# A block with adaptive norms, a gated scan and routed experts: three more expert tiles chosen from the counts after six of eight groups

## Chip, cores and metric

One Trainium2 chip, one core. The metric is the device time of one execution in microseconds (us), lower is better. PE is TensorE, DVE VectorE, ACT ScalarE, POOL GpSimd and SP SyncE.

## What is computed

x has 2 sequences of 2048 tokens with 128 features, so 4096 tokens. With the modulation vectors sa, ca, ga, sb, cb, gb from silu(c) @ wmod:

```
h = layernorm(x) * (1 + ca) + sa
x = x + ga * scan(h)                      # gated linear recurrence along a sequence
h = layernorm(x) * (1 + cb) + sb
logits = silu(h @ rw1 + rb1) @ rw2 + rb2  # 8 experts
two largest logits, softmax over these two -> we[token, expert]
out = sum over e of we[:, e] * (silu(h @ w1[e] + b1[e]) @ w2[e] + b2[e])
x = x + gb * out
```

HID is 512. Every token goes to two experts, so 8192 rows pass through an expert.

## The kernel before

**Groups and tiles.** The first part works in 8 groups of 512 tokens: norm (`norm1`), transpose (`turn_x`), gates, scan, transpose back (`turn_y`), residual and second norm, transpose (`turn_h`), router (`router`, `logits`, `sum`), the two largest (`top2`) and the place of each row (`rank`, `place`). POOL then sends the rows of a group to `sorted_rows` in HBM, ordered by expert, with 8 indirect transfers per group (`send:n` in the plan, two token blocks each; L556, 64 in all). The second part works in 39 tiles of 256 rows of one expert each. For tile s, SP loads the rows into one of U = 10 row places of `xr` (L421); PE turns them (`tx`, L1234), DVE copies them to `xT` (L1010) and copies the expert's weights to a working place (`w1` L1019, `w2` L1028, each after reading the expert's number from `tab` into a register); PE does layer 1 (`l1`, L1245), ACT the silu (`hid`, L665), PE layer 2 (`l2`, L1263), ACT the bias (`yb`, L674), PE turns back (`ty`, L1273), DVE scales (`sc`, L1036) and POOL scatters the rows to `expert_out` with two indirect transfers (`scat`, L567). A load into a used row place waits until the scatter of the tile ten before it has landed (L420).

**Which tiles when.** `tab` holds the first row and the expert of each tile. The first EARLY = 9 tiles hold whole tiles that are full once the first four groups are counted: `early_table` (table1, L944) picks them on DVE, and SP loads them behind the sends of groups 0 to 3 (L434 to L438). The rest are listed by `late_table` (table2, L982), `turn_table` on PE (`tturn`) and `table_row` (table3), from counts at four levels: what is left of the first half (`entries`, table1b), groups 5 and 6 (`middle_levels`, table1c, which reads `lev:0` of PE) and everything. SP then writes padding rows behind each expert (L442), waits for the second table and for all sends (L443 to L445) and loads tile 9 and on.

**What sets the order.** The strings of PLAN (L259) give each engine's order, part by part, from the start of the kernel to tile 10 or so. Each engine executes its parts in that order and waits on semaphores. On DVE, parts joined by + take turns, and `link` (L711) makes the next operation of a part wait for the end of the one before. The PE parts around the change wait as follows: `tx:3` writes the bank that `xT:2` reads, so it waits for it; `logits:7` writes the bank of `lev:0`, so it waits for the first operation of table1c (s_levr); `l1:2` needs `xT:2` and `w1:2`. `turnb` (L1099) transposes the expert biases; it waits for the three transfers of `smallb`, issued by ACT at the start (L583 to L585), and for DVE's copy of the first transpose. `warm:n` are matmuls whose result nobody reads.

After the plan, `expert_steps` (L364) runs a loop of 2 rounds of U = 10 tiles from tile FIRST = 11, then the last 8 tiles as straight code. In that straight part the output is summed group by group: SP loads both rows of each token of a group from `expert_out` (`load_y`), DVE combines them with x in three operations (`combine`, L1050), SP stores. SUMS (L371) says behind which step each group is combined.

## Time and profile before

| | us |
|---|---|
| three runs, median (lowest, highest) | 289.26 (288.16, 289.66) |
| the profiled execution, its own time | 288.93 |
| its span | 287.2 |
| PE busy, share of span | 254.2, 89% |
| DVE busy | 188.9, 66% |
| ACT busy | 166.9, 58% |
| POOL busy | 170.0, 59% |

Busy time is what the profiler sees of each engine; a wait is charged to the work that ended last before it. The span counts from the first to the last instruction; the time around it is 1.7 us. PE's share is an average: the slices of the page show it at nine tenths or more from about the fifteenth of forty on, and lower before, when the groups' scan and norms are made. The lines in the rows are those of the kernel before.

### The profile page before, as it was taken

To read this page: it belongs to the slowest core of one execution; us is meant where nothing else is said; L and a number is where in the kernel's file an instruction comes from. 1 tells how busy PE (TensorE), PEld (TensorE's weight loads), DVE (VectorE), ACT (ScalarE), POOL (GpSimd) and SP (SyncE) were. 2 spreads that over 40 slices of the span, in tenths; PEclk is the share of its full clock that TensorE was granted. 3 is DMA by queue.
4 is the path that set the end of the run, shared out by engine and by line. 5 is a ranking of instruction groups with operands and counts; after the bars stand their busy time and mean duration, and the time that the engine had idled before them with its cause. 6 is when DMAs were issued, how large, how long until landed. Compare 5 with 4: busy or idle time off the path is not lost.

```text
span 287.2 us, 4973 instructions
## 1 busy us (share of the span) xinstructions
PE 254.2 (89%) x1187; PEld 177.0 (62%) x1187; DVE 188.9 (66%) x751; ACT 166.9 (58%) x323; POOL 170.0 (59%) x192
## 2 busy tenths in 40 slices
PE   7886997998889997999998999999999999989910
PEld 3343443354244334787877888888888888867800
DVE  3959999999999987576443444444444446868333
ACT  4169999999885445544554555555555555444400
POOL 3994311267777757777777777545554545635650
PEclk9999999999999999999999999999999999999975
DMA  7994010121131226413423433222216822290504
GB/s 212 306 333 126 19 38 26 51 66 59 46 119 54 88 74 154 126 48 111 141 71 107 110 102 110 53 76 75 65 55 194 237 74 74 75 265 4 160 0 146
DMA packets 45365, 30.51 MB, mean 106 GB/s; under 512 B 5085, under 2 KB 41999, under 8 KB 45342
## 3 DMA queue, kind: packets, MB, share of 16 engines
q1 hardware_dynamic: 39888, 21.49, 27.5%
q0 software_dynamic: 4544, 8.47, 8.9%
q10 hardware_dynamic: 910, 0.30, 0.4%
q8 instruction: 8, 0.13, 0.2%
q14 instruction: 15, 0.12, 0.1%
HBM read 16.39 MB, written 12.67 MB: 101 GB/s over the span
## 4 chain that ended last, share of the span: by engine, by line
PE 43%; POOL 23%; issue 14%; DVE 12%; DMA 5%; DVEq 1%; ACT 1%; POOLq 0%; ACTq 0%; SPq 0%
POOL sorted_rows L556 21%; PE bank L1263 18%; PE bank L1245 17%; PE bank L1273 3%; PE bank L1234 2%; DVE st L722 2%; DMA expert_out<-shared,tx 2%; PE bank L1150 1%; POOL shared L520 1%; PE bank L1151 1%; PE bank L1090 1%; DVE tx L816 1%; DVE hT L821 1%; DVE shared L742 1%; DMA xs<-in_L_attn_x_dram 1%
## 5 line engine op out<-in xcount | busy, mean ns | idle before, releaser
L567 POOL DMA_INDIRECT expert_out<-shared,tx x78 | 79.3, 1016 | 54.1 <-DVE shared L1036 37.6
L665 ACT ACTIVATE hT<-bank,w_t 128x256 f32<-128x256 f32 x156 | 65.5, 471 | 29.5 <-PE bank L1245 28.6
L556 POOL DMA_INDIRECT sorted_rows<-rows,sloti x64 | 64.1, 1001 | 27.2 <-issue 18.3
L1263 PE MATMUL bank<-hT,w_t 128*128 128x256 f32 x312 | 74.1, 380 | 0.0
L1245 PE MATMUL bank<-xT,w_t 128*128 128x256 f32 x312 | 74.0, 380 | 0.0
L1245 PEld LDWEIGHTS bank<-xT,w_t 128*128 128x128 f32 x312 | 56.3, 190 | 6.6 <-DVE w_t L1019 0.5
L1263 PEld LDWEIGHTS bank<-hT,w_t 128*128 128x128 f32 x312 | 56.2, 190 | 6.3
L674 ACT ACTIVATE yT<-bank,w_t 128x256 f32<-128x256 f32 x38 | 18.0, 474 | 46.3 <-PE bank L1263 46.3
L1174 PE MATMUL bank<-h2T,rw_s 128*128 128x512 f32 x64 | 33.5, 623 | 1.0 <-ACT qv L652 0.5
L1010 DVE COPY xT<-bank 128x256 f32<-128x256 f32 x39 | 16.4, 422 | 22.4 <-PE bank L1234 22.4
L1036 DVE TENSOR_TENSOR shared<-bank,tx 128x256 f32<-128x256 f32 x38 | 16.1, 424 | 19.7 <-PE bank L1273 19.6
L1028 DVE COPY w_t<-w_s 128x513 f32 x39 | 17.8, 457 | 16.5 <-issue 15.6
L1019 DVE COPY w_t<-w_s 128x516 f32 x39 | 17.3, 443 | 16.1 <-issue 14.9
L1114 PE MATMUL bank<-ident 128*128 128x512 f32 x30 | 17.7, 702 | 2.0 <-POOL ident L492 2.0
L722 DVE BATCH_NORM_STATS2 st<-xs 128x6 f32<-128x128 f32 x64 | 15.7, 282 | 4.5 <-DMA xs<-in_L_attn_x_dram 4.4
L1174 PEld LDWEIGHTS bank<-h2T,rw_s 128*128 128x128 f32 x64 | 10.0, 189 | 12.6 <-issue 5.9
L1234 PE MATMUL bank<-ident,tx 128*128 128x128 f32 x78 | 15.2, 276 | 2.1 <-DMA tx<-sorted_rows 1.4
L1273 PE MATMUL bank<-ident,yT 128*128 128x128 f32 x76 | 14.7, 275 | 1.9 <-DVE xT L1010 1.5
L1234 PEld LDWEIGHTS bank<-ident,tx 128*128 128x128 f32 x78 | 10.4, 141 | 8.0 <-issue 2.5
L1273 PEld LDWEIGHTS bank<-ident,yT 128*128 128x128 f32 x76 | 10.1, 141 | 7.4 <-issue 4.2
L652 ACT ACTIVATE qv<-bank,smallbT 128x512 f32<-128x512 f32 x16 | 10.8, 686 | 6.4 <-PE bank L1174 6.4
L512 POOL TENSOR_TENSOR rs<-ve,half_neg 128x4 f32<-128x4 f32 x8 | 8.6, 1087 | 9.4 <-DVE ve L729 9.4
(198 smaller groups left out, 326.6 us busy)
## 6 DMA issues: line engine op xcount, KB each, us to landing
tx<-sorted_rows SPq DMA_DIRECT2D x39, 130.0 KB, 2.3
w_s<-in_L_ffn_w_dram SPq DMA_DIRECT2D x16, 256.0 KB, 6.0
xs<-in_L_attn_x_dram SPq DMA_DIRECT2D x8, 256.0 KB, 5.3
rows<-rows SPq DMA_DIRECT2D x8, 256.0 KB, 2.6
av<-expert_out SPq DMA_DIRECT2D x8, 256.0 KB, 3.7
qv<-expert_out SPq DMA_DIRECT2D x6, 256.0 KB, 5.3
expert_out<-shared,tx POOLq DMA_INDIRECT x78, 2.4
sorted_rows<-padr SPq DMA_DIRECT2D x9, 130.0 KB, 2.8
```

The costliest lines, as they stand in the source:

```text
L556: p.indirect_dma_start(sorted_rows[:, :], bass.IndirectOffsetOnAxis(ap=sloti[:, k, t:t + 1], axis=0), rows[:, t, k, :], None).then_inc(s_d ...
L567: p.indirect_dma_start(expert_out[:, :], bass.IndirectOffsetOnAxis(ap=xr_i[:, s % U, n, D + 1:D + 2], axis=0), yo[:, s % U, n, :], None, b ...
L665: ins = nc.scalar.activation(hsT[:, u % 2, h, :], bank[4 + q][:, (h % 2) * SL:(h % 2 + 1) * SL], ACT.Silu, bias=w1_t[:, u % 2, HID + h:HID ...
L674: nc.scalar.activation(yT[:, u % 2, :], out_bank(s)[:, 0:SL], ACT.Identity, bias=w2_t[:, u % 2, HC * D:W2E]).then_inc(s_yT_e, 1)
L722: ins = v.bn_stats(st[:, t, :], xs[:, t, :])
L1028: v.tensor_copy(w2_t[:, u % 2, :], w2_s[:, bass.ds(e * W2E, W2E)]).then_inc(s_w2t, 1)
L1114: t.matmul(bank[to][:, :].rearrange("p (k q) -> p k q", q=P), ident[:, :], ident[:, :].unsqueeze(1).to_broadcast([P, 512 // P, P]), start= ...
L1174: t.matmul(bank[2 + n % 2][:, :], rw1_s[:, h * P:(h + 1) * P], h2T[:, g % 2, :], start=True, stop=True).then_inc(s_rl1, 1)
L1234: ins = t.transpose(bank[1][:, n * P:(n + 1) * P], xr[:, u, n, 0:D], ident[:, :])
L1245: ins = t.matmul(bank[4 + h // 2][:, (h % 2) * SL:(h % 2 + 1) * SL], w1_t[:, u % 2, h * P:(h + 1) * P], xT[:, u % 2, :], start=True, stop= ...
L1263: ins = t.matmul(out_bank(s)[:, 0:SL], w2_t[:, u % 2, h * D:(h + 1) * D], hsT[:, u % 2, h, :], start=(h == 0), stop=(h == HC - 1))
L1273: ins = t.transpose(bank[1][:, n * P:(n + 1) * P], yT[:, u % 2, n * P:(n + 1) * P], ident[:, :])
```

## The change

- SLOTS = 12 row places instead of 10. Tiles 0 and 1 use places 10 and 11, tiles 2 to 9 their own number, 10 and 11 places 0 and 1; from tile 12 on a tile uses its number modulo 10, as before. Places 10 and 11 are used once.
- Tiles 9, 10 and 11 (NEXT = 3) are picked by a table of their own, `middle_table` (tablem), from the counts after six groups (`count6`, copied in `place:6` from a new matmul in `rank:6`). `remaining` (tablen) takes them out of the entries of the last table. Both stand on DVE between w1:1 and table1c. table1c now compares one level instead of two.
- SP loads tiles 9 to 11 behind the sends of groups 4 and 5 (s_disp[1]), ahead of the padding. The last table, the padding and the other sends (s_disp[2]) are waited for ahead of tile 12. The loop starts with tile 12, and 7 tiles follow it.
- The plan is longer by one tile; in it DVE does xT:12 and w1:12 ahead of w2:10.
- On PE, turnb:0 moves from behind gates:0 to the place ahead of warm:1 and mod:0.
- Groups 0 to 5 are summed at steps 32 to 36 and 38; before, at steps 31 to 36. Group 6 stays at step 40.

The diff, without the places where `s % U` only becomes `slot(s)` and `(u + 1) % U` becomes `step_slot(s, u, 1)`:

```diff
-    FIRST = 11
+    FIRST = 12
+    SLOTS = 12
...
-    LATE = TILES - EARLY
+    LATE = TILES - FIRST
+    NEXT = FIRST - EARLY
...
-        yo = shared[:, 0:U * SL].rearrange("p (u n d) -> p u n d", u=U, d=D)
+        yo = shared[:, 0:SLOTS * SL].rearrange("p (u n d) -> p u n d", u=SLOTS, d=D)
...
-        xr = tx[:, 0:U * HALVES * ROW].rearrange("p (u n r) -> p u n r", u=U, n=HALVES)
+        xr = tx[:, 0:SLOTS * HALVES * ROW].rearrange("p (u n r) -> p u n r", u=SLOTS, n=HALVES)
...
+        s_disp = sems("s_disp0", "s_disp1", "s_disp2")
...
+        def counted_6():
+            return bank[6][:, 2 * GT * NE + NE:2 * GT * NE + 2 * NE]
...
-                warm:0 turnc:0 warm:1 mod:0 warm:2 turn_x:0 gates:0 turnb:0 turn_x:1 gates:1 turn_x:2 warm:3 turn_x:3
+                warm:0 turnc:0 turnb:0 warm:1 mod:0 warm:2 turn_x:0 gates:0 turn_x:1 gates:1 turn_x:2 warm:3 turn_x:3
...
-                tx:11 l1:10 ty:8 l2:9""",
+                tx:11 l1:10 ty:8 l2:9 tx:12 l1:11 ty:9 l2:10""",
...
-                norm2:7 place:4 table1:0 w1:0 top2:5 place:5 xT:0 xT:1 w2:0 table1b:0+top2:6 place:6 w1:1 table1c:0
-                w1:2 xT:2 xT:3 w1:3 w2:1 rowsB:0 sc:0 w2:2 top2:7 xT:4 w1:4 place:7 w2:3 sc:1 w1:5 xT:5 w2:4 table2:0
-                sc:2 w1:6 xT:6 sc:3 xT:7 w2:5 w1:7 w2:6 sc:4 w2:7 xT:8 table3:0 sc:5 w1:8 w1:9 sc:6 w2:8 xT:9 w2:9
-                w1:10 xT:10 sc:7 xT:11 w1:11 sc:8 w2:10""",
+                norm2:7 place:4 table1:0 w1:0 top2:5 place:5 xT:0 xT:1 w2:0 table1b:0+top2:6 place:6 w1:1 tablem:0
+                tablen:0 table1c:0 w1:2 xT:2 xT:3 w1:3 w2:1 rowsB:0 sc:0 w2:2 top2:7 xT:4 w1:4 place:7 w2:3 sc:1 w1:5
+                xT:5 w2:4 table2:0 sc:2 w1:6 xT:6 sc:3 xT:7 w2:5 w1:7 w2:6 sc:4 w2:7 xT:8 table3:0 sc:5 w1:8 w1:9 sc:6
+                w2:8 xT:9 w2:9 w1:10 xT:10 sc:7 xT:11 w1:11 sc:8 xT:12 w1:12 w2:10 w2:11 sc:9""",
...
-                hid:4 yb:3 hid:5 yb:4 hid:6 yb:5 hid:7 yb:6 hid:8 yb:7 hid:9 yb:8 hid:10""",
+                hid:4 yb:3 hid:5 yb:4 hid:6 yb:5 hid:7 yb:6 hid:8 yb:7 hid:9 yb:8 hid:10 yb:9 hid:11""",
...
+        def counted_7():
+            return turn_bank("lev", 0)[:, 0:NE]
...
         SUMS = {FIRST + ROUNDS * U: 0, FIRST + ROUNDS * U + 1: 1, FIRST + ROUNDS * U + 2: 2,
-                FIRST + ROUNDS * U + 3: 3, MID + 12: 4, FIVE + 5: 5, TILES + 1: 6}
+                FIRST + ROUNDS * U + 3: 3, FIRST + ROUNDS * U + 4: 4, TILES - 1: 5, TILES + 1: 6}
...
-            return (s - u) // U + 1
+            if static(s) and s < SLOTS:
+                return 1
+            return (s - u) // U + 1 if u >= SLOTS - U else (s - u - U) // U + 1
+
+        def step_slot(s, u, by):
+            return slot(s + by) if static(s) else (u + by) % U
+
+        def slot(s):
+            return U + s if s < SLOTS - U else s % U
 
         def landed(eng, last):
-            for u in range(U):
-                eng.wait_ge(s_sc[u], 16 * HALVES * ((last - u) // U + 1))
+            for u in range(SLOTS):
+                eng.wait_ge(s_sc[u], 16 * HALVES * len([s for s in range(last + 1) if slot(s) == u]))
...
-                if not (static(s) and s < U):
+                if not (static(s) and s < SLOTS):
...
-                if s * HALVES * ROW + HALVES * ROW > GPB * G and s * HALVES * ROW <= GPB * G:
+                if s == 0:
                     sp.wait_ge(s_y, NG)
-                load(s, s % U)
+                load(s, slot(s))
+
+            sp.wait_ge(s_tab, 2)
+            sp.wait_ge(s_disp[1], 16 * TOPK * GPB // 2 * GT)
+            for s in range(EARLY, FIRST):
+                load(s, slot(s))
 
             sp.wait_ge(s_pads, 1)
             for e in range(NE):
                 padding(bass.ds(sp.value_load(pad_i[0:1, e:e + 1], min_val=e * REG, max_val=e * REG + TOK), SL))
-            sp.wait_ge(s_tab, 2)
+            sp.wait_ge(s_tab, 3)
             sp.wait_ge(s_pad, 16 * (NE + 1))
-            sp.wait_ge(s_disp[1], 16 * TOPK * GPB * GT)
-            for s in range(EARLY, FIRST):
-                load(s, s % U)
+            sp.wait_ge(s_disp[2], 16 * TOPK * GPB // 2 * GT)
...
-                            rows[:, t, k, :], None).then_inc(s_disp[t // (GPB * GT)], 16)
+                            rows[:, t, k, :], None).then_inc(s_disp[max(0, t // GT - GPB + 2) // 2], 16)
...
+                if g == 6:
+                    yield from link(v.tensor_copy(count6[:, :], counted_6()))
...
+                v.memset(mbase[:, 2 * NE:2 * NE + 1], float(4 * NE * REG))
+                yield from link(v.memset(mval[:, 1, :], 1.0))
+                v.memset(mval[:, 1, NE - 1:NE], float(1 - NE))
...
-                yield from link(v.tensor_tensor(row_0[:, 0:1], row_p[:, 0:1], base[:, 0:1], ALU.add))
+
+            def middle_table(_):
+                yield from link(v.tensor_tensor(cmpk[:, :, :, :], count6[:, :].unsqueeze(2).unsqueeze(3)
+                                                .to_broadcast([P, NE, 2, KT]), kthr[:, :, :, :], ALU.is_gt))
+                v.tensor_copy(mbase[:, 0:NE], base[:, 0:NE])
+                yield from link(v.tensor_reduce(reach6[:, :, :], cmpk[:, :, :, :], AX.X, ALU.add))
+                yield from link(v.tensor_tensor(low[:, :], full[:, :, 0], reach6[:, :, 1], ALU.min))
+                v.tensor_tensor(more[:, 0:NE], low[:, :], taken[:, :], ALU.subtract)
+                v.scalar_tensor_tensor(mbase[:, NE:2 * NE], low[:, :], float(SL), ereg[:, :], ALU.mult, ALU.add)
+                yield from link(v.tensor_tensor(more[:, NE:2 * NE], reach6[:, :, 1], low[:, :], ALU.subtract))
+                v.tensor_tensor(mval[:, 0, :], mbase[0:1, 1:2 * NE + 1], mbase[0:1, 0:2 * NE], ALU.subtract)
+                yield from link(v.tensor_tensor_scan(mupto[:, :], one[:, 0:2 * NE], more[:, :], 0.0, ALU.mult, ALU.add))
+                yield from link(v.scalar_tensor_tensor(mval[:, 0, :], more[0:1, :], -float(SL), mval[:, 0, :], ALU.mult, ALU.add))
+                yield from link(v.tensor_tensor(cmpm[:, :, :], tauf[:, 0:NEXT].unsqueeze(2).to_broadcast([1, NEXT, 2 * NE]),
+                                                mupto[0:1, :].unsqueeze(1).to_broadcast([1, NEXT, 2 * NE]), ALU.is_ge))
+                yield from link(v.tensor_tensor(cmpn[:, :, :, :], cmpm[:, :, :].unsqueeze(1).to_broadcast([1, 2, NEXT, 2 * NE]),
+                                                mval[:, :, :].unsqueeze(2).to_broadcast([1, 2, NEXT, 2 * NE]), ALU.mult))
+                yield from link(v.tensor_reduce(tfm[:, :, :], cmpn[:, :, :, :], AX.X, ALU.add))
+                yield from link(v.tensor_scalar(tfm[:, 0, :], tfm[:, 0, :], mbase[0:1, 0:1], None, ALU.add))
+                v.tensor_tensor(tab[:, :, EARLY:FIRST], tfm[:, :, :], taus[:, :, 0:NEXT], ALU.add).then_inc(s_tab, 1)
+                dve.wait_ge(s_tab, 2)
+
+            def remaining(_):
+                yield from link(v.scalar_tensor_tensor(tk[:, :], mupto[:, :], -1.0, more[:, :], ALU.mult, ALU.add))
+                yield from link(v.tensor_scalar(tk[:, :], tk[:, :], float(NEXT), 0.0, ALU.add, ALU.max))
+                yield from link(v.tensor_tensor(tk[:, :], tk[:, :], more[:, :], ALU.min))
+                v.tensor_tensor(nent[:, 0:NE], nent[:, 0:NE], tk[:, 0:NE], ALU.subtract)
+                v.tensor_tensor(nent[:, NE:2 * NE], reach6[:, :, 0], full[:, :, 0], ALU.subtract)
+                yield from link(v.scalar_tensor_tensor(base[:, 0:2 * NE], tk[:, :], float(SL), base[:, 0:2 * NE], ALU.mult, ALU.add))
+                v.tensor_tensor(row_0[:, 0:1], row_p[:, 0:1], base[:, 0:1], ALU.add)
+                yield from link(v.tensor_tensor(nent[:, NE:2 * NE], nent[:, NE:2 * NE], tk[:, NE:2 * NE], ALU.subtract))
 
             def middle_levels(_):
                 dve.wait_ge(s_lev, 1)
-                v.tensor_tensor(cmpl[:, :, :, :], levels_of("lev").rearrange("p (l e) -> p l e", l=2).unsqueeze(3)
-                                .to_broadcast([P, 2, NE, KT]),
-                                kthr[:, :, 0, :].unsqueeze(1).to_broadcast([P, 2, NE, KT]), ALU.is_gt).then_inc(s_levr, 1)
+                v.tensor_tensor(cmpl[:, :, :], counted_7().unsqueeze(2).to_broadcast([P, NE, KT]),
+                                kthr[:, :, 0, :], ALU.is_gt).then_inc(s_levr, 1)
                 dve.wait_ge(s_levr, 1)
-                yield from link(v.tensor_reduce(reach[:, :, :], cmpl[:, :, :, :], AX.X, ALU.add))
-                v.tensor_tensor(nent[:, NE:2 * NE], reach[:, 0, :], full[:, :, 0], ALU.subtract)
-                v.tensor_tensor(nent[:, 2 * NE:3 * NE], reach[:, 1, :], reach[:, 0, :], ALU.subtract)
-                yield from link(v.scalar_tensor_tensor(base[:, 2 * NE:NENT].rearrange("p (l e) -> p l e", l=2), reach[:, :, :],
-                                            float(SL), ereg[:, :].unsqueeze(1).to_broadcast([P, 2, NE]),
-                                            ALU.mult, ALU.add))
+                v.scalar_tensor_tensor(base[:, 2 * NE:3 * NE], reach6[:, :, 0], float(SL), ereg[:, :], ALU.mult, ALU.add)
+                yield from link(v.tensor_reduce(reach[:, :], cmpl[:, :, :], AX.X, ALU.add))
+                v.tensor_tensor(nent[:, 2 * NE:3 * NE], reach[:, :], reach6[:, :, 0], ALU.subtract)
+                yield from link(v.scalar_tensor_tensor(base[:, 3 * NE:NENT], reach[:, :], float(SL), ereg[:, :], ALU.mult, ALU.add))
                 yield from link(v.tensor_tensor(dbase[:, :], base[:, 1:NENT + 1], base[:, 0:NENT], ALU.subtract))
...
-                v.tensor_scalar(tab[:, :, EARLY:TILES], table_bank().rearrange("p (k s) -> p k s", k=2),
+                v.tensor_scalar(tab[:, :, FIRST:TILES], table_bank().rearrange("p (k s) -> p k s", k=2),
                                 float(NE * REG), None, ALU.min).then_inc(s_tab, 1)
-                dve.wait_ge(s_tab, 2)
+                dve.wait_ge(s_tab, 3)
...
+                if g == 6:
+                    t.matmul(counted_6(), ones_h[:, :], mboth[:, 6, 0, :], start=True, stop=True)
...
-                t.matmul(levels_of("lev").rearrange("p (l e) -> p l e", l=2), ones_h[:, :], mboth[:, 6:8, 0, :],
-                         start=True, stop=True).then_inc(s_lev, 1)
+                t.matmul(counted_7(), ones_h[:, :], mboth[:, 7, 0, :], start=True, stop=True).then_inc(s_lev, 1)
...
-                        layer2(s - 1, (u - 1) % U, lambda: turn_out(s - 2, (u - 2) % U))
+                        layer2(s - 1, step_slot(s, u, -1), lambda: turn_out(s - 2, step_slot(s, u, -2)))
```

## Rows read from the trace of the kernel before

**Rows 1.** The page, part 4: the chain that ended last, shares of the span by line.
```profile
POOL sorted_rows L556 21%; PE bank L1263 18%; PE bank L1245 17%; PE bank L1273 3%; PE bank L1234 2%; DVE st L722 2%; DMA expert_out<-shared,tx 2%; PE bank L1150 1%; POOL shared L520 1%; PE bank L1151 1%; PE bank L1090 1%; DVE tx L816 1%; DVE hT L821 1%; DVE shared L742 1%; DMA xs<-in_L_attn_x_dram 1%
```

**Rows 2.** The chain in order of time: start us, us, what.
```profile
122.92 1.06 POOL sorted_rows L556
...
144.82 1.00 POOL expert_out L567
...
149.22 2.36 DMA tx<-sorted_rows
```

**Rows 3.** Timeline of PE: start us, us, instruction, idle time before it and releaser.
```profile
119.03 1.06 PE L1181 MATMUL bank<-qv,rw_s 128*32 128x512 f32 x8
...
120.11 0.41 PE L1234 MATMUL bank<-ident,tx 128*128 128x128 f32 x2
...
150.03 0.38 PE L1234 MATMUL bank<-ident,tx 128*128 128x128 f32 x2
...
151.62 0.44 PE L1234 MATMUL bank<-ident,tx 128*128 128x128 f32 x2 [1.21 <-DMA tx<-sorted_rows]
...
151.90 1.89 PE L1245 MATMUL bank<-xT,w_t 128*128 128x256 f32 x8
...
155.79 1.89 PE L1245 MATMUL bank<-xT,w_t 128*128 128x256 f32 x8
```

**Rows 4.** Windows, 120.1 to 150: length, busy PE, PEld, DVE, ACT, POOL, clock, DMA.
```profile
120.10:150.00 29.90, 29.09 (x154) 24.48 (x155) 17.60 (x61) 15.75 (x37) 22.78 (x24) 1.00 0.30 92
```

**Rows 5.** Timeline of DVE around the tables.
```profile
116.62 0.43 DVE L1019 COPY w_t<-w_s 128x516 f32 x1 [0.89 <-issue]
...
116.97 0.42 DVE L970 TENSOR_TENSOR cmpl<-bank,kthr 128x256 f32<-128x256 f32 x1
...
117.42 0.42 DVE L974 TENSOR_REDUCE reach<-cmpl 128x16 f32<-128x256 f32 x1
...
118.03 0.17 DVE L977 SCALAR_TENSOR_TENSOR base<-reach,ereg 128x16 f32<-128x16 f32 x1
...
118.24 0.19 DVE L980 TENSOR_TENSOR dbase<-base 128x32 f32<-128x32 f32 x1
...
119.21 0.43 DVE L1019 COPY w_t<-w_s 128x516 f32 x1 [0.78 <-ACT hT L665]
...
119.55 0.42 DVE L1010 COPY xT<-bank 128x256 f32<-128x256 f32 x1
...
128.31 0.22 DVE L888 TENSOR_REDUCE sloti<-picked 128x8 int32<-128x64 f32 x1
```

**Rows 6.** Timeline of the head, and of PE at 21 to 29 us.
```profile
3.27 0.34 ACTq L585 DMA_DIRECT2D smallb<-in_L_ffn_b_dram  x1
...
4.15 2.08 PE L1114 MATMUL bank<-ident 128*128 128x512 f32 x2
...
9.59 1.11 PE L1090 MATMUL bank<-ident,shared 128*128 128x128 f32 x4 [0.37 <-POOL shared L520]
...
21.35 1.02 PE L1114 MATMUL bank<-ident 128*128 128x512 f32 x2
...
28.39 0.66 PE L1090 MATMUL bank<-ident,hT 128*128 128x128 f32 x4 [2.19 <-DVE hT L821]
```

**Rows 7.** DMA issues: count, KB each, us to landing.
```profile
wa_c<-in_L_attn_w_a_dram ACTq DMA_DIRECT2D x1, 8.0 KB, 4.1
```

**Rows 8.** Timeline of PE in the tail.
```profile
241.48 1.89 PE L1245 MATMUL bank<-xT,w_t 128*128 128x256 f32 x8
...
245.65 1.89 PE L1245 MATMUL bank<-xT,w_t 128*128 128x256 f32 x8
```

**Rows 9.** Timeline of DVE in the tail.
```profile
245.72 0.69 DVE L1056 TENSOR_TENSOR av<-av,gbB 128x512 f32<-128x512 f32 x1
...
271.70 0.43 DVE L1036 TENSOR_TENSOR shared<-bank,tx 128x256 f32<-128x256 f32 x1 [0.88 <-PE bank L1273]
```

**Rows 10.** Timeline of POOL in the tail.
```profile
272.41 0.98 POOL L567 DMA_INDIRECT expert_out<-shared,tx  x1 [0.54 <-DVE shared L1036]
```

More of the change, by code:

```diff
@@ L162, in adaln_block @@
         cmpk = sb("cmpk", [P, NE, 2, KT])
-        cmpl = sb("cmpl", [P, 2, NE, KT])
+        cmpl = sb("cmpl", [P, NE, KT])
         full = sb("full", [P, NE, 2])
-        reach = sb("reach", [P, 2, NE])
+        reach = sb("reach", [P, NE])
+        reach6 = sb("reach6", [P, NE, 2])
+        low = sb("low", [P, NE])
+        count6 = sb("count6", [P, NE])
+        more = sb("more", [P, 2 * NE])
+        mbase = sb("mbase", [P, 2 * NE + 1])
+        mupto = sb("mupto", [P, 2 * NE])
+        mval = sb("mval", [1, 2, 2 * NE])
+        cmpm = sb("cmpm", [1, NEXT, 2 * NE])
+        cmpn = sb("cmpn", [1, 2, NEXT, 2 * NE])
+        tfm = sb("tfm", [1, 2, NEXT])
+        tk = sb("tk", [P, 2 * NE])
         upto1 = sb("upto1", [P, NE])
@@ L224, in adaln_block @@
             "s_dlt", "s_tdl", "s_slot", "s_cnt", "s_tab", "s_pads", "s_pad")
-        s_disp = sems("s_disp0", "s_disp1")
-        s_xr = sems(*(f"s_xr{i}" for i in range(U)))
+        s_disp = sems("s_disp0", "s_disp1", "s_disp2")
+        s_xr = sems(*(f"s_xr{i}" for i in range(SLOTS)))
         s_txp, s_xT, s_w1t, s_w2t, s_l1, s_hs, s_l2, s_yT_e, s_yturn, s_yo, s_fin = sems(
@@ L230, in adaln_block @@
         s_out = sem("s_out")
-        s_sc = sems(*(f"s_sc{i}" for i in range(U)))
+        s_sc = sems(*(f"s_sc{i}" for i in range(SLOTS)))
         s_y01 = sems(*(f"s_y01_{g}" for g in range(NG)))
@@ L987, in late_table @@
                 yield from link(v.tensor_reduce(nent[:, 3 * NE:NENT], cmpk[:, :, 0, :], AX.X, ALU.add))
-                yield from link(v.tensor_tensor(nent[:, 3 * NE:NENT], nent[:, 3 * NE:NENT], reach[:, 1, :], ALU.subtract))
+                yield from link(v.tensor_tensor(nent[:, 3 * NE:NENT], nent[:, 3 * NE:NENT], reach[:, :], ALU.subtract))
                 v.scalar_tensor_tensor(val2[:, 0, :], nent[:, :], -float(SL), dbase[:, :], ALU.mult, ALU.add)
```

44 lines of the change are left out of this document (21 added, 23 removed).

## The prediction

> **What bounds the kernel now.** I read the chain that ended last first. Its largest entry is not TensorE but POOL's row transfers, L556, with 21% of the span [rows 1]. In order of time it shows why: POOL sends all 64 row transfers, then scatters tile 0 at 144.82; only when that scatter has landed can SP refill its row place, and the load for tile 10 starts at 149.22 and takes 2.36 us [rows 2]. Then I read TensorE (PE) around that point. It turns tile 9's rows at 150.03 and tile 10's at 151.62, having been idle for 1.21 us, and layer 1 of tile 9, which stands behind tile 10's turn in its order, starts at 151.90; a normal tile takes 3.89 us [rows 3]. So POOL wins the chain by a nose: in the 29.9 us before the junction PE is busy for 29.09 us [rows 4]. Everything the change can gain at this place is between 150.03 and 151.90. The third view is DVE ahead of that stretch, because the new table is built there. DVE's small operations come in a chain, and tile 2's weights and rows (w1:2, xT:2) start right behind table1c, at 119.21 and 119.55 [rows 5]. PE turns tile 3 at 120.11 [rows 3], when xT:2 has emptied the bank (119.97): in this place PE follows DVE with no slack.
>
> **The change, part by part.**
>
> *Earlier tiles.* Tiles 9 to 11 are loaded after the sends of groups 4 and 5. The 48th send starts at 122.92 [rows 2], so they are in SBUF near 131, long before 150, and all twelve places are free without a scatter. The 1.21 us wait goes. PE still has to turn tile 9, let DVE copy it (0.4 us), turn tile 10 and only then start layer 1: about 1.15 us from turn to layer 1 instead of the 1.87 of now [rows 3]. Gain 0.7 us; bounds 0 and 1.87. Next late is tile 12. It waits for the scatter of tile 2, the fifth and sixth after the sends. From 122.92 to 144.82 POOL made 17 steps of 1.29 us [rows 2], so the sixth ends near 152.5, has landed near 155 and the tile is in SBUF near 157.5. PE wants it two tiles after tile 10, past 159. No wait.
>
> *The new table, on DVE.* `middle_table` and `remaining` stand between w1:1 and table1c, so they are ahead of w1:2 and xT:2. I cost them by the neighbours in [rows 5]. A comparison of 128x256 costs 0.45 us to the next (116.97 to 117.42), a dependent small operation 0.21 (118.03 to 118.24), an independent one 0.08; operations on one partition with 48 to 96 elements lie between the small and the wide ones by their size. The middle table: 0.45 and 0.45 for the wide comparison and reduction, 0.08 for a copy, 0.2 (low), 0.36 (three, one linked), 0.33 (mval and the scan), 0.2, then 0.22, 0.33, 0.25 for the one-partition comparison, product and sum, and 0.2 twice: 3.3 us. `remaining` has eight operations, five with a link: 1.2 us. The copy of the sixth group's count inside place:6 is one more link, 0.2. table1c becomes half as wide in two operations: minus 0.3. In all 4.4 us more ahead of w1:2. **PE stalls by this much.** PE's order there is l1:1, logits:7, tx:3. logits:7 waits for the comparison of table1c, which now comes behind both new parts, and tx:3 waits for xT:2. The two wait in parallel, and the later one, xT:2, moves from 119.55 to about 124.0. From 120.1 to 150 PE has 0.8 us of idle time in all [rows 4], so nothing there takes the delay back, and DVE keeps its order and moves with it. Bounds: 2.3 (below) and 4.9 (a slower scan, longer sequencer gaps).
>
> What one row shows of this cost: the link at 118.03 needs 0.21 us, longer than the operation's own 0.17 [rows 5]. The Trainium skill (Perfetto Trace Analysis, "Optimizing Scalar/DVE Operations") says that a profiled latency is about twice the engine-busy time, because the write acknowledgement overlaps with the next instruction. By that the table would cost about half, an estimate of 2.3 us, and the sum would be 292.1 us. Dependent instructions cannot overlap it, and here most are dependent, so I take the rows.
>
> Who else waits: group 7's place:7 moves by 4.4 us, from the end at 128.5 [rows 5] to 132.9, and POOL wants it for its 57th send, eight sends of 1.29 us before 144.82, at 134.5. It just holds; the sends end as before. SP's padding and the last table move too, and are needed only for tile 12.
>
> *turnb moved to the head.* PE's second transpose goes ahead of warm:1 and mod:0. It waits for smallb, whose last transfer is issued at 3.27; wa_c on the same queue took 4.1 us to land [rows 6, 7]. So it lands at about 7.3 (no sooner than 5.3, DVE's copy, on which turnb also waits). The work behind it took from 4.15 to 9.59 less a wait of 0.37, or 5.1 us [rows 6], so the first turn_x begins at about 12.4 instead of 9.59. That is 2.8 us late (0.8 at the early end), and ACT and DVE are chained to it. Part comes back: PE's pairs of 512 columns took 2.08 us at 4.15 and 1.02 at 21.35 [rows 6], that is 1.2 and then 2.4 GHz by their lengths, while the granted-clock column reads full for both. If the change of speed stays at its time, gates:1, two such pairs or some 4 us at the slow level, runs at the fast one and gives up to 2 us back. The 0.26 us of turnb at its old place goes too. I take 0.9 us net; bounds 0 and 2.8.
>
> *Slots, sums and the end of the plan.* xT:12 and w1:12 stand before w2:10, so layer 2 of tile 10 waits some 0.2 us (0 to 0.4). The sums of the output groups, three DVE operations of about 0.7 us each [rows 9], move from steps 31 to 36 to steps 32 to 36 and 38. A step with a sum takes 4.17 us (241.48 to 245.65) against 3.89 [rows 3, 8]; one fewer gives 0.3 back. But the sixth now stands ahead of the scaling of tile 37, at 271.70 [rows 9], and holds it by 0.9; its scatter follows at 272.41 [rows 10], and the last tile's scatters queue behind it on POOL: 0.8 longer. Net 0.5; bounds minus 1.5 (were the two long sequencer gaps of that tail to vanish) and 1.1. The extra count on PE is one matmul of 8 columns inside rank:6, and the constants gain three small settings on DVE: 0.1 at most, within the bounds above.
>
> **Sum**, against the profiled execution: 288.93 (span 287.2 and 1.7 around it) + 4.4 + 0.9 - 0.7 + 0.2 + 0.5 = 294.2 us. That execution is 0.33 us under the median of 289.26, so the two bases do not differ for this purpose.
>
> **The rivals.**
> - *The head costs all of it.* The change of clock moves with PE's work instead of keeping its time, and nothing is given back: 2.8 for 0.9, so 296.1. For it: at 28.39 PE waits for DVE [rows 6], so what reaches DVE late stays late. Against: the early bound for smallb. Chance 0.15.
> - *A cheap table.* Short one-partition operations overlap and the extra is 2.3 to 3: about 292.5. Chance 0.14.
> - *The clock falls.* logits:7 starts at 119.03 now [rows 3]; PE would stand still from about 119.2 to 122.2 and again for a microsecond before tx:3. The longest gap in the fast part of the trace now is 2.19 us, at 28.39, and the work behind it is still fast [rows 6]. A longer one could bring 1.2 GHz: ten microseconds of work at the slow level cost 5 more, 299. The Trainium skill (TensorE: Matmul & The Clock Gate, "The HAM clock gate") has such a rule, that an idle stretch halves the clock; no row of this trace shows it in the middle of the kernel. Chance 0.08.
> - *Faster: DVE's time is hidden.* If PE had 4.4 us of other work at 120, or DVE reached table1c early, only the gain would be left: minus 0.7 to 1.2 at the junction, minus 0.3 in the tail, so 287.6. It decides as soon as PE's stall before tx:3 is under about 1 us. Against it stands the row at 120.11, 0.14 behind the end of xT:2. Chance 0.05.
> - *It changes next to nothing.* Stall and head come out small, or the loads of 9 to 11 are held back by SP's order, and junction and stall offset each other: 289 to 290.5. Chance 0.08.
>
> **How the numbers follow.** The forecast has 0.50, and 294.2 is its time. The measurement can tell 0.5% from no change, that is 1.45 us about 289.26. Under 287.8 only the hidden case falls: faster 0.05. Between 287.8 and 290.7, same: 0.08. The rest, 0.87, is slower. The range goes from 290.5, the cheap table with a free head, to 297.5, the full head with the upper bounds; it leaves out the falling clock, the hidden case and most of the nothing case, about 0.2.
>
> **What would show it.** DVE's w1:2 starts 4 to 5 us later behind its w1:1 than the 2.6 us of now; PE has two new idle pieces before tx:3, with DVE as releaser; tiles 9 to 11 are loaded near 127 to 131 and the 1.21 us wait is gone; turnb runs near 7 us and the first turn_x after 11. The tail from the last layer 1 to the end is up to 0.8 us longer. I am wrong if w1:2 follows w1:1 within 5 us, if PE is full between 119 and 125, or if the first turn_x is still at 9.6.

## The result and the profile after

The changed kernel takes 297.99 us (median of 6 runs, 295.91 to 299.71), the kernel before beside it 289.0 us (6 runs): a ratio of 1.0302 with a 95% interval of 1.0239 to 1.0365. It is slower, as forecast, but by 8.7 us by the ratio where 5 were forecast, and just above the range of 290.5 to 297.5. A ratio here is not the quotient of the two medians, which can differ from it by a few tenths of a per cent. The profiled execution took 297.64 us; its span is 295.9, against 287.2.

The page of the changed kernel: part 2's row for the granted clock, and the first line of part 4, the chain by engine.

```profile
PEclk9999999999999999958999999999999999999975
...
PE 51%; DVE 33%; issue 5%; DMA 4%; DVEq 2%; ACT 1%; ACTq 1%; POOL 1%; SPq 1%; POOLq 0%
```

POOL, whose row transfers alone were 21% of the chain [rows 1], is left with 1%: the scatters no longer decide when tile 10 is loaded. DVE has a third of the chain. And there is a dip in the clock in two of the 40 slices, at 126 to 141 us. DVE's timeline of the changed kernel, from w1:1 to xT:2, answers to [rows 5]:

```profile
117.82 0.43 DVE L1078 COPY w_t<-w_s 128x516 f32 x1 [0.53 <-issue]
118.17 0.42 DVE L1000 TENSOR_TENSOR cmpk<-count,kthr 128x256 f32<-128x256 f32 x1
...
121.45 0.21 DVE L1021 SCALAR_TENSOR_TENSOR tk<-mupto,more 128x16 f32<-128x16 f32 x1
...
122.75 0.29 DVE L1032 TENSOR_TENSOR cmpl<-bank,kthr 128x128 f32<-128x128 f32 x1
...
124.72 0.45 DVE L1078 COPY w_t<-w_s 128x516 f32 x1 [0.78 <-DVE dbase L1039]
125.09 0.40 DVE L1069 COPY xT<-bank 128x256 f32<-128x256 f32 x1
```

The middle table takes 3.28 us (118.17 to 121.45, where `remaining` starts), `remaining` 1.30 (to 122.75), and w1:2 follows w1:1 by 6.90 us instead of 2.59 [rows 5]: 4.31 more. PE's timeline over the same stretch, answering to [rows 3]:

```profile
118.34 1.96 PE L1305 MATMUL bank<-xT,w_t 128*128 128x256 f32 x8
123.19 1.07 PE L1240 MATMUL bank<-qv,rw_s 128*32 128x512 f32 x8 [2.88 <-DVE cmpl L1032]
125.64 0.66 PE L1294 MATMUL bank<-ident,tx 128*128 128x128 f32 x2 [1.39 <-DVE xT L1069]
126.09 3.62 PE L1305 MATMUL bank<-xT,w_t 128*128 128x256 f32 x8
...
131.50 3.69 PE L1323 MATMUL bank<-hT,w_t 128*128 128x256 f32 x8
135.03 0.38 PE L1294 MATMUL bank<-ident,tx 128*128 128x128 f32 x2
135.25 1.89 PE L1305 MATMUL bank<-xT,w_t 128*128 128x256 f32 x8
```

The two new idle pieces (2.88 and 1.39 us) are there with DVE as their releaser. But behind them eight matmuls of layer 1 take 3.62 us at 126.09 and 1.89 at 135.25: the same work, at half the speed. PE's windows (length, busy, granted clock as a share of 2.4 GHz, DMA share, GB/s) say the same:

```profile
118.00:124.00 6.00, 3.12 (x19) 1.00 0.35 99
124.00:126.00 2.00, 0.61 (x6) 0.69 0.20 67
126.00:134.00 8.00, 8.00 (x26) 0.50 0.37 100
134.00:136.00 2.00, 2.00 (x9) 0.75 0.17 58
136.00:144.00 8.00, 8.00 (x47) 1.00 0.20 60
```

For some ten microseconds, from about 125 to 135, the granted clock is 1.2 GHz; ahead of that PE had stood idle for 4.3 of the 5.3 us between 120.3 and 125.64. The Trainium skill (TensorE: Matmul & The Clock Gate, "HAM oscillation — how this bites in real kernels") warns of such a case, that work behind an idle stretch starts at the low clock; the trace agrees, with 3.62 against 1.89.

The junction in the changed kernel, again answering to [rows 3]: tiles 9 and 10 are turned, and layer 1 of tile 9 starts.

```profile
158.90 0.38 PE L1294 MATMUL bank<-ident,tx 128*128 128x128 f32 x2
159.89 0.41 PE L1294 MATMUL bank<-ident,tx 128*128 128x128 f32 x2 [0.61 <-DVE xT L1069]
160.13 1.89 PE L1305 MATMUL bank<-xT,w_t 128*128 128x256 f32 x8
```

The wait for the transfer is gone; SP issued the loads of tiles 9 to 11 at 127.07 to 129.33. From turn to layer 1 it is 1.23 us instead of 1.87. The head, answering to [rows 6]: turnb, the first turn_x, and the first pair of 512 columns that is fast:

```profile
7.51 0.30 PE L1161 MATMUL bank<-ident,smallb 44*128 44x44 f32 x1 [3.29 <-DMA smallb<-in_L_ffn_b_dram]
...
12.60 1.06 PE L1149 MATMUL bank<-ident,shared 128*128 128x128 f32 x4
...
20.21 1.12 PE L1209 MATMUL bank<-hT,wx_bd 128*128 128x512 f32 x2 [1.07 <-ACT hT L627]
```

turn_x is 3.0 us late; the first tile's turn, at 110.68 against 109.47, only 1.21. Three rows of the kernel before (tile 0 and tile 4 turned, layer 1 of the last tile) and two of the changed kernel (the first and the last of these) are needed beside those shown:

```profile
109.47 0.42 PE L1234 MATMUL bank<-ident,tx 128*128 128x128 f32 x2
...
124.93 0.38 PE L1234 MATMUL bank<-ident,tx 128*128 128x128 f32 x2
...
269.56 1.89 PE L1245 MATMUL bank<-xT,w_t 128*128 128x256 f32 x8
```

```profile
110.68 0.42 PE L1294 MATMUL bank<-ident,tx 128*128 128x128 f32 x2
...
278.28 1.89 PE L1305 MATMUL bank<-xT,w_t 128*128 128x256 f32 x8
```

The profiles side by side, as the lateness of the changed kernel's milestones:

| milestone | before | after | late |
|---|---|---|---|
| tile 0 turned | 109.47 | 110.68 | 1.21 |
| tile 3 turned | 120.11 | 125.64 | 5.53 |
| tile 4 turned | 124.93 | 135.03 | 10.10 |
| tile 9 turned | 150.03 | 158.90 | 8.87 |
| layer 1 of tile 9 | 151.90 | 160.13 | 8.23 |
| layer 1 of tile 37 | 263.67 | 272.02 | 8.35 |
| layer 1 of tile 38, the last | 269.56 | 278.28 | 8.72 |
| end | 287.2 | 295.9 | 8.7 |

Head 1.2; DVE's table 4.3; slow clock 4.6, of which 1.2 comes back by tile 9 (most of it the 0.8 us for which PE stood idle there before [rows 4]; DVE is ahead of it now); junction minus 0.6; from there to layer 1 of the last tile 0.5, and behind that nothing.

### The profile page after: what moved, and what is told of

It reads as the page before. It is cut to its first block, busy times and chain, and to the rows that moved or that the text cites. A ratio compares the mean times of both kernels' runs of the same rounds, so it can differ in the third digit from the quotient of the medians.

```text
span 295.9 us, 5007 instructions
## 1 busy us (share of the span) xinstructions
PE 256.3 (87%) x1188; PEld 180.5 (61%) x1188; DVE 191.6 (65%) x777; ACT 166.7 (56%) x323; POOL 169.0 (57%) x192
## 4 chain that ended last, share of the span: by engine, by line
PE 51%; DVE 33%; issue 5%; DMA 4%; DVEq 2%; ACT 1%; ACTq 1%; POOL 1%; SPq 1%; POOLq 0%
PE bank L1323 20%; PE bank L1305 20%; PE bank L1333 3%; DVE rows L867 3%; PE bank L1294 3%; DVE rows L874 3%; DVE st L749 3%; DVE hT L848 2%; DVE xs L854 2%; DVEq L1062 2%; PE bank L1173 2%; DVE tx L843 2%; DMA smallb<-in_L_ffn_b_dram 1%; DVE shared L769 1%; DVE tx L835 1%
## 5 line engine op out<-in xcount | busy, mean ns | idle before, releaser
L1323 PE MATMUL bank<-hT,w_t 128*128 128x256 f32 x312 | 75.9, 387 | 0.1
L1305 PE MATMUL bank<-xT,w_t 128*128 128x256 f32 x312 | 75.7, 386 | 0.0
L1323 PEld LDWEIGHTS bank<-hT,w_t 128*128 128x128 f32 x312 | 57.3, 194 | 7.1 <-DVE w_t L1087 0.3
L1305 PEld LDWEIGHTS bank<-xT,w_t 128*128 128x128 f32 x312 | 57.5, 194 | 6.7 <-DVE w_t L1078 0.2
L1087 DVE COPY w_t<-w_s 128x513 f32 x39 | 16.8, 432 | 15.7 <-issue 14.6
```

The costliest lines, as they stand in the source:

```text
L1305: ins = t.matmul(bank[4 + h // 2][:, (h % 2) * SL:(h % 2 + 1) * SL], w1_t[:, u % 2, h * P:(h + 1) * P], xT[:, u % 2, :], start=True, stop= ...
L1323: ins = t.matmul(out_bank(s)[:, 0:SL], w2_t[:, u % 2, h * D:(h + 1) * D], hsT[:, u % 2, h, :], start=(h == 0), stop=(h == HC - 1))
```

## The experiments

A clock that falls and a stall that is longer are hard to tell apart in one profile, and so are a head and a table that may interact. So each was tried alone. Ratios are against the kernel before on the same chip, with 95% intervals; the chips and the executions of the kernel before differ between some of them, so that differences of two ratios are less certain than either. The diffs are cut down to the place that matters.

**1. turnb alone.** The kernel before with turnb moved to the head.

```diff
-  warm:0 turnc:0 warm:1 mod:0 warm:2 turn_x:0 gates:0 turnb:0 turn_x:1
+  warm:0 turnc:0 turnb:0 warm:1 mod:0 warm:2 turn_x:0 gates:0 turn_x:1
```

> The kernel before with turnb:0 alone moved to its new place. If the head delay is passed on whole, as the profile of the changed kernel suggests (its first tile's turn is 1.2 us late), this is 1.2 us slower than before, ratio 1.004. If the fast clock only moves along with it: 2.8 us, 1.010. If the plan behind the head absorbs it: 1.000.

Measured 291.07 us (12 runs), 1.0049 [1.0016, 1.0081]: 1.4 us by the ratio, 2.0 by the two medians. In its profile:

```profile
8.48 0.30 PE L1102 MATMUL bank<-ident,smallb 44*128 44x44 f32 x1 [4.26 <-DMA smallb<-in_L_ffn_b_dram]
...
153.55 0.41 PE L1234 MATMUL bank<-ident,tx 128*128 128x128 f32 x2 [0.61 <-DVE xT L1010]
```

smallb was usable a microsecond later than in the changed kernel's profile, and the first tile's turn came at 111.91, 2.4 us late. The end was 1.8 late. The second row says where the difference went: tile 10's turn, which waited 1.21 us for its transfer [rows 3], now waits 0.61 for DVE. PE is 2.5 us late there, but the transfer only 1.8: this delay reaches POOL too (its first scatter starts at 147.04 instead of 144.82), and SP issues the load at 151.04 instead of 149.22. **When PE is later by some 0.6 us more than the transfer is, tile 10's load is on time without any change** (an estimate, 1.21 less 0.61). A delay that moved both alike would leave the wait where it is; experiment 2 has delays that reach PE far more than the transfer.

**2. The stall alone.** The kernel before with 21 dependent small operations on DVE between w1:1 and table1c (the long gap), and with 9 (the short gap); nothing else of the change.

```diff
+            def gap(_):
+                for _ in range(21):
+                    yield from link(v.tensor_tensor(spare[:, :], taken[:, :], ereg[:, :], ALU.add))
```

> The kernel before with a chain of 21 dependent small DVE operations (8 columns, into a tile that nobody reads) between w1:1 and table1c, some 4.3 us, and nothing else. Theory: DVE's delay there and the fall of PE's clock behind it are nearly the whole loss, so PE idles for about 2.8 and 1.4 us, runs tile 2 at 1.2 GHz, and the kernel takes 289 + 4.3 + 4 - 1.2 (the wait at 150 us is swallowed) = 296, ratio 1.024. Rival (the loss comes from the longer code, the row places or SP's order, not from this gap): under 1.010.

> The kernel before with 9 instead of 21 dependent small operations on DVE between w1:1 and table1c, some 1.9 us. Theory (the time is PE's stall, then the clock if the stall is long): PE idles 0.3 to 0.6 and 1.4 us, the clock stays up, the tiles reach the junction 1.9 us later and the wait of 1.2 us there is swallowed: plus 0.7 to 1.3, ratio 1.003 to 1.004. Rival (loss in proportion to the gap, 0.21 us each as in the full gap's 4.6 for 21): plus 2.0, 1.007.

The long one took 293.67 us (4 runs), 1.0121 [1.0065, 1.0177]; the short one 289.88 (10 runs), 1.0027 [0.9995, 1.006]. PE with the long one:

```profile
122.28 1.06 PE L1186 MATMUL bank<-qv,rw_s 128*32 128x512 f32 x8 [2.76 <-DVE cmpl L971]
124.91 0.66 PE L1239 MATMUL bank<-ident,tx 128*128 128x128 f32 x2 [1.56 <-DVE xT L1015]
125.37 3.62 PE L1250 MATMUL bank<-xT,w_t 128*128 128x256 f32 x8
...
130.46 1.97 PE L1268 MATMUL bank<-hT,w_t 128*128 128x256 f32 x8
```

and with the short one:

```profile
119.15 1.07 PE L1186 MATMUL bank<-qv,rw_s 128*32 128x512 f32 x8 [0.26 <-DVE cmpl L971]
121.77 0.41 PE L1239 MATMUL bank<-ident,tx 128*128 128x128 f32 x2 [1.56 <-DVE xT L1015]
122.02 1.89 PE L1250 MATMUL bank<-xT,w_t 128*128 128x256 f32 x8
...
152.35 0.41 PE L1239 MATMUL bank<-ident,tx 128*128 128x128 f32 x2 [0.61 <-DVE xT L1015]
```

Idle for 2.76 and 1.56 us, PE goes on at half speed; idle for 0.26 and 1.56, at full speed. The slow stretch comes from the idle time on PE, not from what the new table computes. Here it lasts some 7 us (from about 123.3 to 130), three less than in the changed kernel. From tile 0's turn to tile 9's it is 6.47 us more than before, 4.68 of them by tile 3, so the slow clock is left with 1.8, where I had put 4. Another 1.2 came back in the tail: layer 1 of tile 9 is 6.0 us late and the end 4.8, and PE's wait of 1.08 us for xT, which the kernel before has at 256.94, is not in this profile. That is why 296 was too much. The short gap puts tile 3's turn 2.0 us later than before, counted from tile 0's, but layer 1 of tile 9 only 1.1: its last row shows tile 10's turn waiting 0.61 us for DVE and no longer for its transfer, and with the long gap it is the same 0.61. So the stall by itself removes the wait that the earlier tiles are to remove.

**3. The stall without the idle time.** The changed kernel, with unread matmuls on PE in the two idle pieces: six and two, then three and one. The lines that give their number and a wait of theirs are not shown; the wait holds nothing up, for the first of them starts as soon as layer 1 of tile 1 is done.

```diff
-                logits:7 tx:3 l1:2
+                warm:10 logits:7 warm:11 tx:3 l1:2
```

> The changed kernel with unread matmuls of 512 columns in the two idle stretches of PE, six ahead of logits:7 and two ahead of tx:3. Theory: the gap on DVE stays (4.3 us), but the clock stays at 2.4 GHz, so 3.5 to 4.5 us come back: about 294, ratio to before 1.016. Rival (the idle time itself costs and the clock is a detail of the profiled run): no gain, 298, 1.030.

> As the run that kept PE busy, but with three and one unread matmuls instead of six and two: each takes 0.87 us, not the 0.43 that I had counted, so six ran 2.4 us past the gap. Theory: tile 3's turn is no later than in the changed kernel (5.5 us behind before) and the clock stays up: 298 - 3.4 = 294.5, ratio 1.019. Rival (the clock falls all the same, or its fall is no cost): 297 or more.

Six and two: 296.03 us, 1.0226 [1.0168, 1.0284]. One unread matmul of 512 columns takes 0.87 us (two matmul instructions each in the timeline), so six and two were too many; tile 3's turn came at 127.14, which is 17.5 us after tile 0's instead of 15.0. Three and one: 295.39 us, 1.0207 [1.016, 1.0253], with this timeline of PE:

```profile
121.27 2.74 PE L1175 MATMUL bank<-ident 128*128 128x512 f32 x6
124.30 1.07 PE L1242 MATMUL bank<-qv,rw_s 128*32 128x512 f32 x8 [0.30 <-DVE cmpl L1032]
125.30 1.13 PE L1175 MATMUL bank<-ident 128*128 128x512 f32 x2
126.76 0.41 PE L1296 MATMUL bank<-ident,tx 128*128 128x128 f32 x2 [0.34 <-DVE xT L1069]
127.01 1.89 PE L1307 MATMUL bank<-xT,w_t 128*128 128x256 f32 x8
```

Nothing useful was added and DVE is as long as it was: from tile 0's turn to tile 3's it is 14.94 us (14.96 without the matmuls). Yet the kernel is faster, since layer 1 of tile 2 takes 1.89 and not 3.62. From tile 0's turn to tile 9's: 40.56 us in the kernel before, 48.22 in the changed one, 44.71 here. **Of 7.66 us lost in that stretch, 3.5 are the clock and 4.15 the stall.** In the measured times the clock is worth 0.95% of the kernel, 2.7 us, by ratios whose intervals overlap a little; the profile has the firmer number.

**4. The same without the moved turnb.** The changed kernel with turnb at its old place, and then also with three and one unread matmuls.

```diff
-  warm:0 turnc:0 turnb:0 warm:1 mod:0 warm:2 turn_x:0 gates:0 turn_x:1
+  warm:0 turnc:0 warm:1 mod:0 warm:2 turn_x:0 gates:0 turnb:0 turn_x:1
```

> The changed kernel with turnb:0 alone put back behind gates:0. The move alone cost 0.5% (1.4 us) in the kernel before. If the head and the gap on DVE add up, this is 298 - 1.4 = 296.6, ratio 1.026. Rival: the two interact (an early head delay shifts where the clock falls and rises), then 294 to 295, the 293.7 of the gap alone.

> turnb at its old place, and three and one unread matmuls in PE's two idle pieces, once more, since the last eight runs found the kernel before at 330 us. If the slow clock costs what the rows of the two profiles show: a ratio of 1.012 to 1.015, against 1.0195 without the unread matmuls. If the clock costs nothing that the end sees: 1.0195.

Without the unread matmuls 293.85 us, 1.0195 [1.0145, 1.0246]; with them 292.96 us, 1.0132 [1.0074, 1.019]. The table and its stall alone so cost some 3.8 us and the clock 1.8 more, by ratios whose intervals overlap; the profiles say it more sharply. Two of the six executions with the unread matmuls took 295.75 and 296.27 us at a mean clock of 0.967 and 0.955, the other four 292.21 to 293.32 at 0.977 to 0.986; their lower mean clock says that it fell somewhere all the same, but neither was profiled. PE without the unread matmuls:

```profile
121.38 1.60 PE L1240 MATMUL bank<-qv,rw_s 128*32 128x512 f32 x8 [2.77 <-DVE cmpl L1032]
123.98 0.66 PE L1294 MATMUL bank<-ident,tx 128*128 128x128 f32 x2 [1.01 <-DVE xT L1069]
124.44 3.62 PE L1305 MATMUL bank<-xT,w_t 128*128 128x256 f32 x8
...
129.24 1.97 PE L1323 MATMUL bank<-hT,w_t 128*128 128x256 f32 x8
```

Here the clock fell while logits:7 ran, and PE was fast again by 129.24. Counted from tile 0's turn, tile 9's is at 45.86 us, and 44.66 with the unread matmuls: 1.2 us for a slow stretch that began early and lay partly under idle time, against 3.5 in 3.

**5. The table without the stall.** The changed kernel with the steps of the new table put one by one between DVE's copies for PE, and logits:7's comparison left right behind w1:1. The last table's steps are spread in the same way, and PE's tturn:0 stands later. First with the moved turnb; then with turnb back, DVE's part for the row gates (rowsB) moved back and spread too, and w2:10 ahead of xT:12; then this last with turnb moved again. The diff shows the place of the stall (two lines of the plan joined, cut short on both sides):

```diff
-  place:6 w1:1 tablem:0 tablen:0 table1c:0 w1:2 xT:2 xT:3 w1:3 w2:1 rowsB:0 sc:0 w2:2
+  place:6 w1:1 levr:0 w1:2 tm:1 xT:2 xT:3 tm:1 w1:3 tm:1 w2:1 tm:1 sc:0 tm:1 w2:2
```

> The changed kernel with the steps of the middle table, the remaining entries, the levels and the last table put one by one between DVE's copies instead of in one piece; only the comparison that logits:7 waits for stays behind w1:1; rowsB moves to behind w2:9 and tturn:0 by one tile. turnb stays early. Theory: PE has work at 119 to 126 us, the clock stays up, what is left is the 1.2 us of the head less 0.6 to 1.2 at the junction: 288.5 to 290, ratio 0.998 to 1.003. Rival (DVE has no room for 5 us of table anywhere in this stretch): 292 or more, 1.010.

> The changed kernel with the tables' steps threaded between the copies, rowsB's steps too, tturn:0 between tx:9 and tx:10, turnb:0 at its old place and w2:10 ahead of xT:12. Theory: no cost of the change is left and its gain is: the turn of tile 10 no longer waits (0.7 us), one summing step fewer (0.3), tail 0.3 longer: minus 0.5 to minus 1.0, ratio 0.9965 to 0.998. Rival (the three early tiles bring nothing that can be measured): 1.000. If it is over 1.003, a cost of the change is still unnamed.

> The threaded table (0.9961) with turnb alone moved to the head, once more. If the head's cost was partly hidden in the kernel before by the wait for tile 10's load, and nothing hides it here: about 1.004. If it costs the same everywhere, 1.4 us: about 1.001.

Measured: 292.34 us, 1.0099 [1.0062, 1.0136]; 288.01 us, 0.9961 [0.9921, 1.0001]; 290.03 us, 1.0003 [0.9969, 1.0037]. In the second one PE has, at the place of the stall and at the junction:

```profile
119.28 0.44 PE L1313 MATMUL bank<-ident,tx 128*128 128x128 f32 x2
...
148.30 0.38 PE L1313 MATMUL bank<-ident,tx 128*128 128x128 f32 x2
...
149.54 1.68 PE L1324 MATMUL bank<-xT,w_t 128*128 128x256 f32 x7
```

Tile 3 is turned at 119.28, so neither stall nor slow clock is left, and all that the earlier tiles can bring is there: the best version takes 288.01 us, 1.1 under the kernel before by the ratio, with an interval that ends at no change, so that a gain is likely but not shown. The moved turnb costs this version 0.42%, or 1.2 us, against the 1.4 of experiment 1. I had expected that it might cost more (2.0 to 2.5), because nothing hides it here; that did not come out, though with 0.4% to either side of each ratio it is not excluded. The first of the three had further small stalls, 0.88 us ahead of tile 8's turn and 1.28 ahead of a turn at 154.73, from where its row gates stood.

**6. Eight runs that settle nothing.** The changed kernel again, the kernel of 4 with PE kept busy, the long gap of 2 with PE kept busy (three and one), and the threaded table with the moved turnb, twice over.

> The changed kernel once more, in the same batch as the three variants below, so that its two costs can be added up on one footing. If table and head add without interaction, the ratio is the sum of the table without the head (1.0195) and the head alone (1.0049), 1.024 or 296.1 us. If they interact (the kernel before had 0.6 us of slack at the wait for tile 10's load, which hides a part of either cost alone but not of both), it is 1.028 to 1.031 again, about 298 us.

> The changed kernel with turnb at its old place and with three and one unread matmuls in the two idle pieces before tile 3's turn. The profile of the same kernel without the unread matmuls shows the clock at half speed for about 6 us and tile 9's turn 1.15 us later, counted from tile 0's, than with them. If the slow clock is what costs this, the time is 1.0 to 1.5 us under that kernel's 293.85: about 292.6, ratio 1.012 to 1.015, and the rest is DVE's table alone. If the clock costs nothing that the end sees, it stays at 1.0195.

> The kernel before with the 21 dependent operations ahead of table1c, as before, now with three and one unread matmuls in PE's idle pieces. No slow clock: tile 9's turn 44.7 us after tile 0's (47.0 without them), and 291.5 us, ratio 1.008 to 1.010, against 1.0121. If the unread matmuls cost as much as the clock, no difference to 1.0121.

> The threaded table without the stall (0.9961), with turnb alone moved to the head. In the kernel before, the first tile's turn came 2.4 us late and the end 1.8, since the 1.21 us wait for tile 10's load took up 0.6. Here tiles 9 to 11 are loaded early and nothing takes it up: if that is the interaction, the cost is 2.0 to 2.5 us, ratio about 1.004; if the head's cost is the same everywhere, 1.4 us, ratio about 1.001.

> The changed kernel once more, since in the last four runs the kernel before itself took 329.87 us. If table (1.0195 without the head) and head (1.0049 alone) only add, the ratio is 1.024; if one takes away what hides the other, 1.028 to 1.031, about 298 us.

> turnb at its old place, and three and one unread matmuls in PE's two idle pieces. If the slow clock costs what the rows of the two profiles show (tile 9's turn 1.15 us later, counted from tile 0's), the ratio is 1.012 to 1.015, against 1.0195 without the unread matmuls; the rest, some 4 us, is DVE's table alone. If the clock costs nothing that the end sees, 1.0195.

> The kernel before with the 21 operations and with PE kept busy by three and one unread matmuls. If half of that kernel's loss was the slow clock: tile 9's turn 44.7 us after tile 0's instead of 47.0 and a ratio of 1.006 to 1.009, against 1.0121. If the loss is the stall alone: 1.012.

> The threaded table (0.9961) with turnb alone moved to the head. If the head's cost was partly hidden in the kernel before by the wait for tile 10's load, and nothing hides it here, 2.0 to 2.5 us: a ratio of about 1.004. If the head costs the same everywhere, 1.4 us: about 1.001.

On these two occasions the kernel before itself took 329.87 and 329.99 us. The ratios were 1.0122, 1.0118, 1.0059 and 1.0106 the first time and 1.0081, 1.0093, 1.0084 and 1.0029 the second, in the order of the list: the changed kernel has 1.0122 and 1.0081 there, not 1.0302. Of the first of them, two rows of ACT:

```profile
128.77 0.69 ACT L679 ACTIVATE qv<-bank,smallbT 128x512 f32<-128x512 f32 x1 [7.34 <-remote]
138.77 1.57 ACT L692 ACTIVATE hT<-bank,w_t 128x256 f32<-128x256 f32 x4 [9.31 <-remote]
```

Single operations last as long as ever (0.69 us for that of 128x512), but ACT and DVE stand still for 4 to 12 us at a time between some 80 and 185 us, in most cases with no engine of this core as the releaser (`remote`). Tile 3 is turned at 148 to 151 us in every version there, after those pauses, so that a stall at this place is no longer what these runs measure. What the pauses are was not found, and neither the costs nor the order of the versions is taken from these ratios; they were set aside after they were seen. The last two kernels of 4 and 5 were then run once more (their results stand there); for the long gap with PE kept busy the question stayed open.

## Why the prediction was wrong in size

**DVE's table: right.** From w1:1 to w1:2 4.31 us more were measured. The sum had 4.2 for this and 0.2 for the copy of the count ahead of w1:1, which does not show: w1:1 is late by 1.20 us, tile 0's turn by 1.21. The small dependent operations follow each other by 0.20 to 0.21 us (21 of them in 4.32 in experiment 2), and the half that the remark of the Trainium skill (Perfetto Trace Analysis, "Optimizing Scalar/DVE Operations") would have given did not come true for a dependent chain.

**Stall on PE: right.** It has the two idle pieces and DVE as releaser; from tile 0's turn to tile 3's it is 4.32 us longer.

**The junction: right, 0.64 of 0.7.** What the forecast did not see, experiment 2 shows: the stall alone would have brought it too, since with either gap, and none of the change, tile 10's turn waits 0.61 us for DVE and not for its transfer. The change pays for a gain that its own cost makes worthless.

**The head: mechanism right, size small.** turn_x is at 12.60 against the 12.4 forecast, 3.0 us late, and at 29.52 instead of 28.39 [rows 6] the lateness is down to 1.1: the pair of 512 columns at 20.21 takes 1.12 us where the one at 19.46 in the kernel before takes 1.62. The cost was 1.2 us in the profile and 1.2 to 1.4 by the ratios of experiments 1 and 5 (2.0 by the medians of 1), against 0.9; that is inside the bounds. It is a mean over unlike executions: in the six undisturbed profiles with turnb early, tile 0 is turned at 109.28 to 111.91, in the six with turnb late at 109.03 to 110.04. By the ratios of 3 and 4 it is more where the stall is there too: 3.1 us (1.0302 against 1.0195), and 2.2 with PE kept busy (1.0207 against 1.0132), each uncertain by about two.

**End of the plan and tail: the size near, the path not, so this is luck.** Layer 2 of tile 10 is held by 0.24 us against the 0.2 forecast (it starts at 170.22 and not the 169.97 of an unhindered one), and the step without a sum gives 0.27 back against 0.3. But the 0.8 for the scatters held behind the sixth sum did not come: the scaling of tile 37 is 9.07 us late (280.77 against 271.70 [rows 9]), 0.35 more than layer 1 of the last tile, and POOL's last scatter, at 285.44 against 276.71, is level with it again. What the tail did lose, 0.37, lies between layer 1 of tile 37 and of tile 38: DVE's copy w2 at 271.40 has 0.70 us of sequencer gap before it where its counterpart at 262.68 has 0.33, and PE then waits 0.45 for xT. The two long sequencer gaps did not vanish.

**The step that failed: the slow clock stood among the rivals, at 0.08, and not in the sum.** All other terms give 294.2, and the profile of the changed kernel, less the 3.3 us net that the clock cost there (4.57 less 1.23 won back), gives 294.3. That these agree to 0.1 us is partly luck, since the head was 0.3 more than its term and table and tail 0.3 less. The reason given against it was one row: the work behind an idle time of 2.19 us at 28.39 was still fast [rows 6]. That was one execution, and one idle piece, shorter than the 3.0 us that I myself forecast, with another microsecond close behind (2.88 and 1.39 measured). A run of experiment 5 shows how weak it was. Its PE timeline at the same place of the kernel (threaded table, turnb early):

```profile
29.38 0.66 PE L1168 MATMUL bank<-ident,hT 128*128 128x128 f32 x4 [2.19 <-DVE hT L849]
29.87 1.78 PE L1228 MATMUL bank<-hT,wx_bd 128*128 128x512 f32 x2
...
35.45 1.02 PE L1228 MATMUL bank<-hT,wx_bd 128*128 128x512 f32 x2
```

The same idle time of 2.19 us, and this time the slow clock behind it (granted 0.50 from 30 to 33 us). It is so in three of the six undisturbed profiles with turnb early (this one, three and one of experiment 3, the first of 5) and in none of the six with turnb late. The rival's own figure, 299, was near: ten microseconds at the slow level cost 4.57 us there, not 5, and 1.23 were won back. With a chance that fitted how little spoke against it, the range would have reached it. The stated bounds of the other terms, with nothing gained at the junction, add up to 298.1 and would have covered the measured time with no clock in them; that would have been luck. None of the three signs of being wrong that the prediction named came up, for none of them looked at the clock.

**What stays open.** The parts measured alone, 3.8 for table and stall, 1.8 to 2.7 for the clock and 1.2 to 1.4 for the head, add up to 6.8 to 7.9 us, against 8.7 for all together (interval 6.9 to 10.5). The intervals of the parts are about a microsecond or more to either side, so that the rest of 0.8 to 1.9 may be nothing; or it is that the slow stretch was longer in the changed kernel (ten microseconds) than with turnb back or with the plain gap (7), which would also make the moved turnb look dear where the stall is. The two profiles fit this: the changed kernel's span is 4.2 us over that with turnb back, 1.6 of them by tile 0's turn (110.68 against 109.06) and 2.4 more by tile 9's (48.22 against 45.86 us from tile 0's). But it is one execution of each, and what sets the length of the slow stretch was not found.

## What to carry to other kernels

When a chain of small operations is put ahead of what a full engine waits for, add up its steps from rows of dependent operations (0.2 us each here); and if the waiting engine is TensorE, ask separately what its clock will do behind the idle time, for that can cost as much again. Short steps between the copies cost nothing that could be measured here, where a block of the same steps costs 4 us and the clock. And before a wait is removed, look how much lateness of the waiting engine would remove it anyway: a wait of 1.2 us, of which 0.6 could be gained, is not worth a chain of 4.
